# Masking the second attention behind its exponential on VectorE, with a new written order of steps

## The reference

```
q = (query @ Wq + bq), k, v = split(key_value @ Wkv + bkv)      # per head
scores = einsum('bhqd,bhkd->bhqk', q, k) * SCALE
scores = where(mask, scores, finfo.min)
attn   = softmax(scores, axis=-1)
out    = einsum('bhqk,bhkd->bhqd', attn, v) ... @ Wo + bo
```

## Time and profile before

| | |
|---|---|
| median of 3 runs | 987.9 us (987.82 to 988.53) |
| profiled execution, span from first to last instruction | 986.1 us |
| busy share TensorE matmul / weight load | 96% / 71% |
| busy share VectorE, ScalarE, GpSimd | 64%, 54%, 22% |
| mean granted TensorE clock | 0.993 of full speed |
| HBM traffic over the span | 56 GB/s |

### The profile page before, as it was taken

How to read it: one execution, slowest core, us unless ns; L and a number is a source line. 1 busy time by engine, 2 the same in 40 slices (tenths; PEclk the granted TensorE clock), 3 DMA queues, 4 the chain that set the end, 5 groups by cost and what they waited for, 6 DMA issues and landing times.

```text
span 986.1 us, 17493 instructions
## 1 busy us (share of the span) xinstructions
PE 949.3 (96%) x6126; PEld 702.7 (71%) x6126; DVE 634.1 (64%) x2245; ACT 536.3 (54%) x1097; POOL 221.5 (22%) x317
## 2 busy tenths in 40 slices
PE   8999999989999999999999999999999999999998
PEld 6665665757687766778687766776686757777777
DVE  4634674675675776867586776775776676736564
ACT  1341644776368643875448644866376544864421
POOL 3104311303240132403141023302321032012210
PEclk9999999999999999999999999999999999999999
DMA  7308535400540023520432104402132004000000
GB/s 261 58 30 226 127 113 113 88 10 17 113 94 9 11 50 70 113 49 13 80 73 46 44 1 86 98 11 49 27 67 59 12 17 92 1 12 1 1 1 22
DMA packets 41078, 58.27 MB, mean 59 GB/s; under 512 B 4096, under 2 KB 35840, under 8 KB 37376
## 3 DMA queue, kind: packets, MB, share of 16 engines
q1 hardware_dynamic: 39600, 48.59, 23.6%
q10 hardware_dynamic: 1392, 8.56, 2.3%
HBM read 41.67 MB, written 13.89 MB: 56 GB/s over the span
## 4 chain that ended last, share of the span: by engine, by line
PE 77%; ACT 9%; DVE 8%; issue 4%; POOL 1%; DMA 1%; ACTq 0%; SPq 0%; DVEq 0%; POOLq 0%
PE bank L1657 11%; PE bank L1984 6%; PE bank L1517 6%; PE bank L1736 6%; PE bank L1714 6%; PE bank L1508 6%; PE bank L1629 4%; PE bank L1995 4%; PE bank L1771 4%; PE bank L1765 3%; PE bank L1717 3%; ACT PT L886 2%; ACT QA L873 2%; PE bank L1797 2%; PE bank L1526 2%
## 5 line engine op out<-in xcount | busy, mean ns | idle before, releaser
L886 ACT ACTIVATE PT<-bank 128x512 f32<-128x512 f32 x256 | 153.0, 598 | 127.4 <-PE bank L1717 71.8
L1657 PE MATMUL bank<-w,xhT 128*128 128x512 f32 x256 | 126.8, 599 | 0.0
L1714 PE MATMUL bank<-QA,KA 104*128 104x256 bf16 x512 | 112.7, 273 | 12.4 <-ACT PT L886 10.5
L1184 DVE CUSTOM_DVE_ANT_0 bank<-bank,maskb 128x256 f32<-128x256 f32 x256 | 101.7, 450 | 25.7 <-PE bank L1629 25.4
L1177 DVE TENSOR_REDUCE mx<-bank 128x2 f32<-128x512 f32 x128 | 83.6, 684 | 28.9 <-PE bank L1629 28.5
L1629 PE MATMUL bank<-KA,QA 96*128 96x256 bf16 x512 | 91.1, 273 | 1.9 <-DVE mx L1184 0.8
L1984 PE MATMUL bank<-xhBT,wi 128*128 128x256 f32 x336 | 87.0, 390 | 2.9 <-DVE hT L1491 2.5
L1714 PEld LDWEIGHTS bank<-QA,KA 104*128 104x128 bf16 x512 | 46.5, 99 | 60.3 <-issue 45.8
L1230 DVE SCALAR_TENSOR_TENSOR x<-bank,one,x 128x256 f32<-128x256 f32 x128 | 61.5, 481 | 21.6 <-PE bank L1657 17.6
L873 ACT COPY QA<-bank 8x256 bf16<-8x256 bf16 (+1 forms) x128 | 67.8, 575 | 10.1 <-PE bank L1695 8.8
L1984 PEld LDWEIGHTS bank<-xhBT,wi 128*128 128x128 f32 x336 | 59.2, 191 | 12.9 <-DVE hT L1491 5.6
(11 more groups left out here) (311 smaller groups left out, 2028.3 us busy)
## 6 DMA issues: line engine op xcount, KB each, us to landing
QA<-scratch SPq DMA_DIRECT2D x90, 128.0 KB, 4.8
scratch<-kparts SPq DMA_DIRECT2D x30, 192.0 KB, 2.4
KA<-scratch SPq DMA_DIRECT2D x15, 384.0 KB, 4.6
scratch<-qparts SPq DMA_DIRECT2D x30, 192.0 KB, 2.3
KA<-scratch SPq DMA_DIRECT2D x15, 256.0 KB, 5.5
w<-pack ACTq DMA_DIRECT2D x1, 2345.0 KB, 8.3
wi<-ipack ACTq DMA_DIRECT2D x1, 2304.0 KB, 8.5
xin<-x_in SPq DMA_DIRECT2D x8, 256.0 KB, 6.3
```

Of the source, the lines that this page charges most:

```text
L886: act.activation(PT[:, n % RING, :, :].rearrange("p t s -> p (t s)"), st_bank[:, :], ACT.Exp).then_inc(exp_s, 1)
L1184: last = dve.tensor_tensor_reduce(s, s, maskb[:, t, :], op0=ALU.add, op1=ALU.max, scale=1.0, scalar=-HUGE, accum_out=mx[:, i % 4, n % GH, ...
L1657: last = pe.matmul(bank[n % 2][:, :], xhT[:, kk, t * P:(t + 1) * P], W("exp0", KT)[:, kk, i * 512:(i + 1) * 512], start=(kk == 0), stop=(k ...
L1714: last = pe.matmul(st_bank[:, t * S:(t + 1) * S], KA[m][0:KM, v, t * P:(t + 1) * P], QA[m][0:KM, v, :], start=True, stop=(m == 0))
```

## The change

The matmul with the identity (L1717) is left out. After ScalarE has written the exponentials of a head of the second attention, VectorE takes the minimum of `PT` with a new tile `keepb`, in place: 3e38 where the mask allows and 0 where it forbids. An allowed weight stays as it is, and a forbidden one, which may be large because the maximum is taken over allowed scores only, becomes exactly 0. `keepb` is made once, from the same loaded mask as `maskb`. `maskb` stays in use for the maxima (L1184). The value matmuls of the second attention wait for the minimum (`kept_s`) instead of the exponential. In VectorE's thread "v" the minimums of 8 heads come ahead of the first division, four more ahead of the second and of the third.

The diff; the strings are cut to their first rows, and "..." marks what is left out:

```diff
--- before.py
+++ after.py
@@ -88,50 +88,52 @@
 
 TURNS = {
     "sync":
-        "pppppppppppppppppsssppbspppppppppppspssppsppppppppppbsssppsppbpppppppppsppsbspsppbpppppppppppbspspsp"
...
+        "pppppbpppppppppppspssspppppppppppppspspspsppppppppppsspbspspppppbppppppppsssbpspppppppppppbppbssppps"
...
     "gpsimd":
-        "ppppppppssppsppsppsssppspssppsppssappsspsssasppaapapbbppbsbpsabssppbapbsaappsapbsbbspbpssabbbppssppp"
...
+        "ppppppppppppssssppsssppspspppsspsspapspsspspssaaapppapbbbsbpbassssbpapaappsapsbbbsppbpbsapbpbassbpss"
...
     "scalar":
-        "pppppppppppvvpvvvpvvvvvvpvvvvvvvvvvvpvpsspsppsbsbpvpvbvvvpvvvvvvpvvvvvvvvsvvvvpbpvbvbbvvvsvbvvvvbvbv"
...
+        "ppppppppppppvvpvvvvvvvvvpvvvvvvvvvvvvpspsspppssvbvppvbvvvsvpvvvbvpvvvvvvvvvvvvbbppvbvbvvvbvbbvbvvvsb"
...
     "vector":
-        "ppppppvppppvppppvssssssssssssssssssssvvpvpvpvspspssssssssssspssssspssssspssssbsssssssssvsssssvsspsvs"
-        "vpsspssvssssssssppsvssssvvvsssvasassssspssssssaaasssspssssspsbsssssssvsvssssssssasaapvsvppsvssppaasa"
-        "aasasaabsbsvsbbbbbvsbbsvssvbbsbvaabssppsssbbssbssaaassbpsbsssbsssssssbsbsssbvssaasvsabssvvsssvaaaaas"
...
+        "pvpvppppppppvppppssssssssssssssssssssvvpvvvppssssssspsspsssspsssssssssspsspssssssssvsbssvbpsvsvsspsp"
+        "ssssvsssspssssspsvvvvvvvvsssvvsvvsvsvvsvsvvssvvsvaasppsssspsssssssaaasssssssssssssssssssvasasasssvsp"
+        "vvspspvsssapavasaaspasvvvvvavsvabsbsvvvvvvbvvbvbvsbbbbvsssvbsbbvaabsssspsspbbsbsssaaapssbsssbssbssbs"
...
     "tensor":
-        "pppwwwppwwwwwwwwwwwwwwwwppwwwwwwwwwwwwpwwwwwpwpwwwwwwppwwwwwwwwwwwwwwwwwwwsswwspspssvsvswwvsvpsvswwv"
-        "ssvpvvssvpsvwwwvvvvwwvpvvvvwwwvpvwwwvvwwwwvpvwwvpvvpwwwwwwwpwspsssssssssssssssssppbspsspbsspssbpssvb"
-        "svsbssvvbvpssvbvpvssvvpssvbvvvvsspvsvvssvvpvswwvsswvvssvpvssvwsvvsspvswvpvvwwvsvsvsvvsvssvspvvvsvsvp"
-        "vvsvvsvsvssvvsvsvsvsvvppwwwswwwsasaaspsspsasvsasvspassvvpvsvassvavvssvavsvspsavspsvsvvspsvvassvpvsps"
...
+        "ppwwwwwwwwwwwwwwwwwwwwwwwwwwwwwwwwwwwwwwpwwppppwwwwwwwwwwwwpwwwpwpwwwwwppwwwwwwwwwwwwwwwwwwwwwwwwwww"
+        "wwwwwwwwwwwwwwwwwwwwwwwwwwwwwwsswwspspsvsspvssvsvsvswvpvwwvsvsvspsvwwvvvvwwvwwwwwvvvvwwvpvpvvwwvwwvw"
+        "wvpvvwwwwwwpwwwwwspsssssssssssssspssspwppwwwswwssppsspsspssvbsvsbsvbvssvbvspsvbvsvpsvpvswwvvvvpbvvvs"
+        "vsvbvpvbsvsvwwvspvswvsvsspsvssvwsvpvsvwvspsvwwvwwvvpvwsvsvssvvvsvssvvsvvssssvssvsssvsvpvwwvpvsvvpssp"
...
 }
@@ -208,6 +210,7 @@
         ident = W("ident")
         identb = sb("identb", [P, P], BF16)
         maskb = sb("maskb", [P, T, S], BF16)
+        keepb = sb("keepb", [P, T, S], BF16)
         bqs = [sb(f"bqs{m}", [P, KT]) for m in range(3)]
         hb4 = sb("hb4", [P, 1])
         hb3 = sb("hb3", [P, 1])
@@ -364,7 +367,7 @@
 
         s_ps, max_s = sem("s_ps"), sem("max_s")
         mq_s, mT_ps, negm_s = sem("mq_s"), sem("mT_ps"), sem("negm_s")
-        st_ps, exp_s = sem("st_ps"), sem("exp_s")
+        st_ps, exp_s, kept_s = sem("st_ps"), sem("exp_s"), sem("kept_s")
         pv_ps, ot_s, otT_ps, att_s = sem("pv_ps"), sem("ot_s"), sem("otT_ps"), sem("att_s")
         attT_ps, attT_s, o_ps, added = sem("attT_ps"), sem("attT_s"), sem("o_ps"), sem("added")
 
@@ -1266,12 +1269,26 @@
                 yield
                 dve.wait_ge(nomask_in, 16)
                 for t in range(T):
-                    last = dve.tensor_copy(maskb[:, t, :], att[:, t, :])
+                    dve.tensor_copy(maskb[:, t, :], att[:, t, :])
+                    last = dve.tensor_scalar(keepb[:, t, :], att[:, t, :], 0.0, HUGE, ALU.is_ge, ALU.mult)
                 last.then_inc(mask_ready, 1)
                 yield
+                def keep(n):
+                    dve.wait_ge(exp_s, n + 1)
+                    dve.tensor_tensor(PT[:, n % RING, :, :], PT[:, n % RING, :, :], keepb[:, :, :], ALU.min
+                                      ).then_inc(kept_s, 1)
+
                 for q, (b, m) in enumerate(ATTENTIONS):
+                    if m == 1:
+                        for n in range(q * H, q * H + 2 * GH):
+                            keep(n)
+                            yield
                     for g in range(ITEMS):
                         i = q * ITEMS + g
+                        if m == 1 and g in (1, 2):
+                            for n in range(q * H + (g + 1) * GH, q * H + (g + 2) * GH):
+                                keep(n)
+                                yield
                         dve.wait_ge(otT_ps, i + 1)
                         if g == 0 and q:
                             dve.wait_ge(attT_ps, q)
@@ -1700,7 +1717,7 @@
                     if q == 0:
                         pe.wait_ge(mask_ready, 1)
                     elif (b, m) == (0, 1):
-                        pe.wait_ge(mask_ready, 3)
+                        pe.wait_ge(mask_ready, 2)
                     tops(q, 0)
                     yield
                     for v in range(H + 4):
@@ -1712,10 +1729,7 @@
                                 pe.wait_ge(exp_s, n)
                             for t in range(T):
                                 last = pe.matmul(st_bank[:, t * S:(t + 1) * S], KA[m][0:KM, v, t * P:(t + 1) * P],
-                                                 QA[m][0:KM, v, :], start=True, stop=(m == 0))
-                                if m == 1:
-                                    last = pe.matmul(st_bank[:, t * S:(t + 1) * S], identb[:, :], maskb[:, t, :],
-                                                     start=False, stop=True)
+                                                 QA[m][0:KM, v, :], start=True, stop=True)
                             last.then_inc(st_ps, 1)
                             yield
                             if v % GH == 1 and v // GH + 1 < ITEMS:
@@ -1731,7 +1745,10 @@
                                     pe.wait_ge(attT_s, q)
                             for g in (2 * pair, 2 * pair + 1):
                                 i = q * ITEMS + g
-                                pe.wait_ge(exp_s, GH * (i + 1))
+                                if m == 0:
+                                    pe.wait_ge(exp_s, GH * (i + 1))
+                                else:
+                                    pe.wait_ge(kept_s, b * H + GH * (g + 1))
                                 for t, h in itertools.product(range(T), range(GH)):
                                     last = pe.matmul(pv_bank[32 * h:32 * h + 32, g % 2 * S:(g % 2 + 1) * S], vflat[m][:, t, (g * GH + h) * VW:(g * GH + h) * VW + 32],
                                                      PT[:, (i * GH + h) % RING, t, :], start=(t == 0), stop=(t == T - 1),
```

More of the change, by code:

```diff
@@ new lines @@
+        "avbvvvvbvaavavvavvaavabpavvsvvvvvvavvavvvvvvbvvvbvpvvbvpsbabsbpaaabappbvvbvvvvvbvvvvbavvvvvbvavbvavv"
+        "avpavavvbvvvpvsvaaavavvvaavvvvvbvvsvbvvsvbcvbabbavaavbavvvbvvabvabvavbvabavavbvvvavaavavbvvvaavbaaba"
+        "aaabaaaaaaaaaaabaaaaaaaaaaaaabbaaaabbccccbbcbcbcbccccccccccccccccccc",
+    "vector":
+        "pvpvppppppppvppppssssssssssssssssssssvvpvvvppssssssspsspsssspsssssssssspsspssssssssvsbssvbpsvsvsspsp"
+        "ssssvsssspssssspsvvvvvvvvsssvvsvvsvsvvsvsvvssvvsvaasppsssspsssssssaaasssssssssssssssssssvasasasssvsp"
+        "vvspspvsssapavasaaspasvvvvvavsvabsbsvvvvvvbvvbvbvsbbbbvsssvbsbbvaabsssspsspbbsbsssaaapssbsssbssbssbs"
+        "sssssbsvsbssasavasbvsvssspsvaaasapabsasvssvavspavbbvvvvbspsbvvbbsbbsbbvvvvvvsvbvbsbpssvbvsssvaabbsps"
+        "bpsspssssssbsaaasbssbsssssbsssbsssssvbsaaavssssssspvvsbsapaasasasvpasbvspvabavpbsbvvvvvbsbbbsbbbsvvv"
+        "vsvvbbsbvvsvsvbvsvsbspvbabassbpssssbsspsbsssbaasssasbsssbssssbvsaaasssssvsbssspvsspvpssbvasaasaassap"
+        "spvvavvabsbvvvvbsbbsbbvbbsvvsvvbvbvsbssvvbvssvsvbbpvabasspsbssspsbsssssaasabssssbssssssssbssvsbsssaa"
+        "asbvsssvvsssssvsabsaavpaasvvavvsvsavbvspabsbvvvvsvbvsvvbvbvbbbbvsvspsbbsvbapapbsbbsbsssasabsssssbssp"
+        "assbsssssbsbvsssssbssvssssvavasassbsvsssssvvsbvvbsvsssavaavavasassasabssbvvvsvvvvbvbvbbvbbbpvvbbbvac"
+        "absscsssbbsssbsssaaavbsvsbssvbvssvbsvvvbaaassbvvvvvbvvaaavavavabvvababvabaaabbbbbbbaaaabbbaaaabaaaaa"
+        "aaaaababaacbacccbcccccbcccccbcccccbccccbcbccccccccccccbcccccccccc",
@@ new lines @@
+    "tensor":
+        "ppwwwwwwwwwwwwwwwwwwwwwwwwwwwwwwwwwwwwwwpwwppppwwwwwwwwwwwwpwwwpwpwwwwwppwwwwwwwwwwwwwwwwwwwwwwwwwww"
+        "wwwwwwwwwwwwwwwwwwwwwwwwwwwwwwsswwspspsvsspvssvsvsvswvpvwwvsvsvspsvwwvvvvwwvwwwwwvvvvwwvpvpvvwwvwwvw"
+        "wvpvvwwwwwwpwwwwwspsssssssssssssspssspwppwwwswwssppsspsspssvbsvsbsvbvssvbvspsvbvsvpsvpvswwvvvvpbvvvs"
+        "vsvbvpvbsvsvwwvspvswvsvsspsvssvwsvpvsvwvspsvwwvwwvvpvwsvsvssvvvsvssvvsvvssssvssvsssvsvpvwwvpvsvvpssp"
+        "wasaasppssavssasvssasvvvspavssvavvassvpvvssvaspssvvassspspvasvsvvvssvsvasvvaavssvpvavavvpavpsvvsvssv"
+        "spvssvvasvasvpvavvvsssvvsbvsvvbvpvpvssvsvsbvbbvpsvvsbsbbsapssbsaasbssbavpasvpabvssvbabvsasvbbsvavvbb"
+        "spsasbvsbvspvvssbvbvspvsbvsbasvpvbvsbbpvabvbvvsabavasvbbvasvasvasvpvsbbvsvvavabvavsvpvsvpvvvvbssbvvs"
```

(11 more changed lines are left out.)

37 lines of the change are left out of this document (7 added, 30 removed).

## The result

The changed kernel takes **1057.2 us** (median of 4 runs, 1056.75 to 1057.43), the kernel before 987.9 beside it: a ratio of 1.071 (95% interval 1.069 to 1.072), 69.3 us slower. I had forecast 981.5 and a range up to 1001. Direction and size were wrong.

The account below looks back on a forecast made before the run. TensorE's queue was taken to set the time. 986.1 - 28.2 (mask matmuls) + 14.1 (start) + 1.1 and 0.7 (other fillers) + 6 (minimums) = 979.8, plus 1.8 around the span: 981.5 us, range 966 to 1001.

Parts of the forecast that it names:

- The order: New strings: start +14.1 us, other early fillers +1.1, late fillers +0.7, queues nothing; other moved steps not costed.
- part 2: Start: two larger filler clusters on TensorE delay the first real scores from 35.32 to 49.4 us, +14.1 (+10 to +17).
- part 4: Queues of SyncE, GpSimd and ScalarE: a few steps shift, bulk work the same; costed at nothing, -1 to +1 us.
- Part 1: Mask matmuls leave TensorE's queue: 256 slots of 0.11 us, 28.2 us less (ends 0 and 63.5).
- the sign that I had named: Part 1 is wrong if the second attention's score groups start no denser and the other parts' sum still holds.
- The steady stretch says it doesn't: Reason for taking 28.2 us: TensorE, busy 589.5 of 600 us from 200 to 800, was not waiting at the mask matmuls.
- The rival that the mask matmuls were hidden: TensorE only waits longer for exponentials, so nothing is saved: 1010 us; chance 0.03, counted with the slower side.
- Part 3: VectorE's 128 minimums, 88.7 us of work: TensorE's waits for VectorE double, +6 us (-3 to +32).
- the 20 that I had named as the sign of an error: TensorE's waits on VectorE, 100 to 900 us, forecast at 9 to 18 us; above 20 us Part 3 is wrong.
- It has the room: VectorE can absorb 16 us of minimums held by GpSimd's lock, 0.13 us each; covered by the +6 and its range.
- VectorE takes TensorE's place: Rival, slower: TensorE waits 0.25 us for each of 128 minimums, 32 us instead of 6, giving 1007 us; chance 0.19.
- The two sides cancel: Rival, within 0.2% of before: GpSimd holds minimums 16 us, two thirds (10.7) reaching TensorE, 986 to 990 us; chance 0.13.

Follow-up runs that it names:

- new-order ladder: Changed kernel's strings: mask matmuls without minimum 1040.3 us; neither 1030.0; one-element copy for the minimum 1028.7; row maximum 1034.9; minimum 1057.2.
- old-order ladder: Strings of the kernel before: unchanged 987.9 us; mask matmuls gone 975.2; plus one-element copy 981.4; row maximum instead 1013.4; minimum instead 1027.7.
- plain insertion: Full masking change with all five strings of the kernel before, the 128 minimums set into VectorE's string about where their exponentials are ready: 1027.7 us.
- the run of SyncE's order: Kernel before with only SyncE's string replaced by the new one, the same transfers in another order: 1003.7 us, ratio 1.016.

## Why the prediction was wrong, point by point

The new-order ladder splits the 75.7 us between 981.5 and 1057.2 (36.5 + 17.9 + 21.2, the rest is rounding).

**The order: forecast +15.9, measured +52.4, an error of 36.5 us.** It is the largest, and a step that stands in the prediction only by what it leaves out. I walked the new strings through the start (part 2), costed the queues at nothing (part 4), and took every other moved step for neutral because each does the same work. For SyncE I said "All their bulk work is the same"; one store moved seven places costs 16 us among the old strings. That loss is not one of the changed kernel's, so the zero may be right there for SyncE, but the reason for it was wrong. The 42 us that remain beside the fillers are placed (most of them behind the masked attentions of the first batches), but not put down to single moves: TensorE waits more for VectorE at many small rows. Which moves do it stays open.

**Part 2, the start: right.** Transposes at 18.30 (18.7 forecast), third attention's first small matmul at 28.19 (28.3), last cluster at 39.47 (37.0), scores at 51.92 (49.4): +16.6 for +14.1, inside the bound of 17. The 2.5 us more arise among the small matmuls, where the granted clock was 0.51 from 30 to 37 us; the kernel before had 1.00 there (22.4 to 31 us).

**Part 1, the mask matmuls: forecast -28.2, measured -10.3, an error of 17.9 us.** The term is mis-sized: it took the price of a slot for the saving at the end. The slots went for the price read in the earlier trace rows, and the sign that I had named (score groups no denser) would not have shown the error. What failed is "The steady stretch says it doesn't". With the matmuls gone in the old order TensorE's waits between 100 and 900 us grow from 16.7 to 24.8 us, by 5.2 on VectorE and 2.9 on ScalarE: 8.1 of the 15.5 us that are missing there. TensorE's idle time over the whole span agrees, 36.8 us before (986.1 - 949.3) and 45.3 after (972.7 - 927.4). The other 7 us are not placed: TensorE's busy time falls by 21.9 us, not by 28.2, and a pause shorter than the modelled end of a matmul does not show as idle. The rival that the mask matmuls were hidden, at 0.03, held more than half of the truth. That ScalarE waits for TensorE does not exclude it, since TensorE also waits in its turn, only at other heads.

**Part 3, the minimum: forecast +6, measured +27.2 (1030.0 to 1057.2), an error of 21.2 us.** I doubled 6.0 us of waits to 12; they became 42.9, beyond the 20 that I had named as the sign of an error. That sign does not tell this part alone, since the new order without any minimum already has 23.9. The waits and the work by themselves cost 4.9 us (1030.0 to 1034.9), close to the +6. I had the lock, at 16 us on VectorE, and let idle time swallow it: it is the term that was put at nothing. Its size on VectorE was near (128 x (831 - 677) ns = 19.7 us); what failed was "It has the room". All of it, 22 us, reached the end. The room was read from means: the 84% busy that I forecast for VectorE between 200 and 800 us puts all 128 minimums there (it is 78%, 467 of 600), while in a masked stretch it is busy 56 of 65 us, and GpSimd, which I let be met at random at 22%, 28 of 65. The Trainium skill, page "SBUF — State Buffer", section "Who interferes with whom", says that a VectorE instruction with two inputs in SBUF contends with a GpSimd instruction that reads SBUF. The traces agree: 1.6 us for a minimum wholly beside GpSimd, and no stretch for the one-input row maximum (677 ns, GpSimd back to 221.5 us).

**The rivals.** "VectorE takes TensorE's place" had the mechanism, VectorE late in a fixed order, with 0.19 and 1007 us. It is what the old-order ladder shows, even for the plain insertion: +52 us for 99 us of VectorE's time, not the 32 of my upper end. In the changed kernel the larger share of the minimum's cost is that of "The two sides cancel": GpSimd's long operations holding minimums. It had 10.7 us reaching TensorE, two thirds of 16; measured were 22.3, all of it. Of the order itself I had no rival.

**The clock** adds to it: 65 us at the lower level against 14. If every one of the 51 us more ran at half pace, 26 us of the 69 are the clock's; that is an estimate of the most, and no run isolates it. The losses stand where TensorE had waited, as in the window 200 to 300 (busy 85.80 of 100, granted 0.91), and as after the 11 us of standing in the run of SyncE's order.

## What to carry to other kernels

In a kernel whose instruction order is written out, a new order is a change of its own: run it alone, with the old work, before costing what it is meant to serve. How much of its idle time an engine at 64% can give depends on the order: 67 us more of occupied time cost 32 us at the end in one order and 6 in the other, so look at its busiest short stretches, not at the mean. The same matmuls that start every 0.11 us returned 0.04 to 0.05 each. Price a removed slot by the next limit of its stretch too, and let a lock between engines count in full unless a wait behind it is shown to be slack.

## What the runs showed of the hardware that I had not expected

A 128x512 minimum with two SBUF inputs and GpSimd's 128x512 operations run in step once they meet: 1.6 us for each minimum and 1.60 us for each of GpSimd's, four of them in a row from 172.86 us on, where alone they take 0.69 and 1.16. A reduction of the same tile at the same places shows none of it. And the lock's price at the end (22 us in one order, 14 in the other) was about what it cost VectorE, 19.7 and 12.3 us (98.9 - 86.6), though VectorE was idle 29% of the time.
